# Chunk inverses: four link buffers, stores regrouped over SP and POOL, gate work moved, and dense products at every step of the joins

## What is computed

```python
T = jnp.where(tri, 0.0, -(kb @ jnp.swapaxes(k, -1, -2)))
for i in range(1, chunk):
    T = T.at[..., i, :].add(jnp.einsum('...j,...jl->...l', T[..., i, :], T))
T = T + jnp.eye(chunk, dtype=T.dtype)
u = T @ v
w = T @ kb
```

```python
ga = (2 * (ga >= 0) - 1) * jnp.maximum(jnp.abs(ga), 0.25)
gb = (2 * (gb >= 0) - 1) * jnp.maximum(jnp.abs(gb), 0.25)
```

## Time and profile before

| | us |
|---|---|
| median of 3 runs | 2583.9 (2582.48 to 2597.81) |
| the profiled execution | 2589.23 |
| its span | 2587.5 |
| PE busy in the span | 2394.4 (93%) |
| DVE busy | 1655.0 (64%) |
| ACT busy | 1109.5 (43%) |
| POOL busy | 616.3 (24%) |

### The profile page before, as it was taken

The page is one execution under the profiler, slowest core; times in us unless marked ns, Lnnn a source line. Parts: engine busy times, 40 slices in busy tenths (PEclk is TensorE's granted clock), DMA queues, the critical chain, the costliest instruction groups (busy, mean ns, idle before and its releaser), DMA issues.

```text
span 2587.5 us, 41994 instructions
## 1 busy us (share of the span) xinstructions
PE 2394.4 (93%) x14594; PEld 1659.7 (64%) x14594; DVE 1655.0 (64%) x4354; ACT 1109.5 (43%) x2350; POOL 616.3 (24%) x417
## 2 busy tenths in 40 slices
PE   6899997667897999979999999999999999999998
PEld 4466665555676888845666666666666666666665
DVE  4487886449922566525767676667667676766675
ACT  2477876346663222224334424433443344244331
POOL 1145554031101111211312231222123132312210
PEclk9999998787667999989999999999999999999999
DMA  5447556978767767421202210220122022101000
GB/s 166 162 149 219 174 166 192 270 212 203 212 155 223 217 204 225 156 74 49 58 1 58 58 50 9 58 58 13 45 59 58 1 58 58 43 15 58 9 9 8
DMA packets 376312, 272.14 MB, mean 105 GB/s; under 512 B 199714, under 2 KB 333794, under 8 KB 373906
## 3 DMA queue, kind: packets, MB, share of 16 engines
q1 hardware_dynamic: 371474, 243.85, 33.6%
q0 software_dynamic: 4640, 25.73, 2.9%
HBM read 168.60 MB, written 100.93 MB: 104 GB/s over the span
## 4 chain that ended last, share of the span: by engine, by line
PE 43%; DVE 9%; issue 3%; POOL 2%; ACT 0%; DMA 0%; DVEq 0%; SPq 0%; POOLq 0%; ACTq 0%
PE mx_dn L2002 16%; PE mx_up L1988 15%; PE mx_m L1938 4%; DVE mx_acc L2316 4%; PE mx_m L1965 2%; POOL mx_rms L1894 2%; PE mx_m L1942 1%; PE mx_m L1979 1%; DVE hl L2224 1%; DVE mx_st L2214 1%; DVE hl L2199 1%; DVE hl L2188 1%; DVE mx_rms L2193 1%; PE mx_m L1973 1%; PE mx_m L1947 1%
## 5 line engine op out<-in xcount | busy, mean ns | idle before, releaser
L2316 DVE SCALAR_TENSOR_TENSOR mx_acc<-mx_dn,mx_comb,mx_acc 128x256 f32<-128x256 f32 x1024 | 424.3, 478 | 356.6 <-PE mx_dn L2002 352.7
L2002 PE MATMUL mx_dn<-mx_edn,mx_hs 128*128 128x256 f32 x2048 | 487.7, 381 | 0.0
L1988 PE MATMUL mx_up<-mx_h2T,mx_eup 128*128 128x512 f32 x1024 | 484.3, 595 | 0.0
L2002 PEld LDWEIGHTS mx_dn<-mx_edn,mx_hs 128*128 128x128 f32 x2048 | 384.4, 190 | 145.6 <-issue 91.0
L2090 ACT ACTIVATE mx_hs<-mx_up 128x512 f32<-128x512 f32 x320 | 190.8, 596 | 625.8 <-PE mx_up L1988 625.1
L1988 PEld LDWEIGHTS mx_up<-mx_h2T,mx_eup 128*128 128x128 f32 x1024 | 190.9, 190 | 156.1 <-issue 145.2
L675 DVE SCALAR_TENSOR_TENSOR cv_acc<-cv_pre,conv_w,cv_acc 128x512 f32<-128x512 f32 x288 | 215.7, 750 | 78.2 <-ACT cv_acc L597 71.3
L539 PE MATMUL cv_pj<-cv_hT,wqkv 128*128 128x512 f32 x384 | 181.8, 604 | 12.7 <-ACT cv_acc L597 7.7
L713 POOL TENSOR_TENSOR rn<-cv_ss,half_pow 128x8 f32 x64 | 127.5, 1992 | 13.2 <-POOL cv_ss L709 13.2
L1880 POOL TENSOR_TENSOR mx_st<-mx_tmp,root_pow 128x24 f32<-128x24 f32 x30 | 124.6, 4168 | 20.1 <-DVE mx_tmp L2142 20.1
L1938 PE MATMUL mx_m<-mx_hT,wr 128*128 128x512 f32 x256 | 122.2, 601 | 3.3 <-DMA mx_x<-_attn_hidden_states_dram 2.5
(11 more groups left out here) (292 smaller groups left out, 3998.7 us busy)
## 6 DMA issues: line engine op xcount, KB each, us to landing
kqT_d<-cv_kqc SPq DMA_DIRECT2D x16, 1024.0 KB, 8.5
vf_d<-cv_vf SPq DMA_DIRECT2D x16, 1024.0 KB, 5.4
fl_toep<-taps_d SPq DMA_DIRECT2D x32, 392.0 KB, 7.3
ds_kqT<-kqT_d SPq DMA_DIRECT2D x10, 1024.0 KB, 5.9
fl_v<-vf_d SPq DMA_DIRECT2D x8, 1216.0 KB
ci_kT<-kqT_d POOLq DMA_DIRECT2D x19, 512.0 KB, 5.7
fl_d<-fl_out POOLq DMA_DIRECT2D x8, 1029.0 KB, 7.2
xin<-_attn_hidden_states_dram SPq DMA_DIRECT2D x16, 512.0 KB, 4.3
```

The costliest lines, as they stand in the source:

```text
L1988: ins = pe.matmul(up_ps[x % 2][:], lhs, h2T[i][:, k, :], start=(k == 0), stop=(k == KD - 1))
L2002: ins = pe.matmul(dn_ps[(i + n) % 2][:, j, :], hs[x % 4][:, j * P:(j + 1) * P], rhs, start=(x == 0 and j % 2 == 0) or x >= NS, stop=(x >= ...
L2316: ins = dve.scalar_tensor_tensor(out=acc[i][:, j, :], in0=dn_ps[(i + n) % 2][:, j, :], scalar=comb[i][:, j, e:e + 1], in1=acc[i][:, j, :], ...
```

## The change

- `link` gets four buffers in place of two, each with its semaphore.
- The order on SP: in the first eight steps, groups of three steps' stores (half, load of k, link), then three loads of blocks, then the fourth step's stores and the fourth load. Steps 8 to 10 are stored, then the blocks of step 12 loaded, then step 11 stored, then the blocks of steps 13 to 15 loaded, then `first_step`, then the halves of steps 12 to 15.
- The links of steps 12 to 15 are stored by POOL, behind its last stores of inverses.
- The loads of Wo and of the norm's weight go from SP's start to POOL, behind the last inverses. The gate work on DVE goes behind the last round of inversion, and `clamp_done` with its wait is dropped.
- The products in front of the four rounds become 30, 8, 8 and 40, all ahead of the wait for blocks. At the first tile of each other step PE waits for the Y copy of the tile before and issues 8.

```diff
-    K3 = 3 * Q
+    BUSY = (30, 8, 8, 40)
...
-        link = [sb(f"ci_link{i}", [P, B, H // 2, DK]) for i in two]
+        link = [sb(f"ci_link{i}", [P, B, H // 2, DK]) for i in range(RB)]
...
-                if p == 1:
-                    sp.wait_ge(clamp_done, 1)
...
-            for q in range(TB):
+            for q in range(0, 2 * ST, ST):
+                for i in range(ST - 1):
+                    put(q + i)
+                for i in range(ST - 1):
+                    load_blocks(q + ST + i)
+                put(q + ST - 1)
+                load_blocks(q + 2 * ST - 1)
+            for q in range(2 * ST, 3 * ST - 1):
+                put(q)
+            load_blocks(3 * ST)
+            put(3 * ST - 1)
+            for q in range(3 * ST + 1, TB):
+                load_blocks(q)
+            first_step()
+            for q in range(3 * ST, TB):
                 put_half(q)
-                if TB + KB + q < TB + 2 * ST:
-                    load_k(TB + KB + q)
-                if (q + RB) % ST == 0:
-                    put_link(q)
-                if q + RB < TB:
-                    load_blocks(q + RB)
-                if (q + RB) % ST:
-                    put_link(q)
-                if q == 3 * ST + 1:
-                    first_step()
...
+            pool.dma_start(prod[1][:].rearrange("p (k n) -> p k n", k=KD), w.Wo.rearrange("(k p) n -> p k n", p=P))\
+                .then_inc(wo_in, 16)
+            for i in two:
+                pool.dma_start(prod[0][i * DK:(i + 1) * DK, 0:1], w.o_norm_w.unsqueeze(1)).then_inc(wo_in, 16)
+            for q in range(3 * ST, TB):
+                put_link(q)
+            pool.wait_ge(last_link_out, 32 * ST)
...
                 if x % BT == 0:
                     if x:
                         pe.wait_ge(Y_done, x)
-                    busy(x, 6)
+                    busy(x, BUSY[x // BT])
+                elif b == 0:
+                    pe.wait_ge(Y_done, x)
+                    busy(x, 8)
                 if b == 0:
                     pe.wait_ge(blocks_in[q % RB], 16 * 6 * (q // RB + 1))
-                if x % BT == 0:
-                    busy(x, 8)
...
-                if b == 0 and q >= 2:
-                    act.wait_ge(link_out[q % 2], 32 * (q // 2))
+                if b == 0 and q >= RB:
+                    act.wait_ge(link_out[q % RB], 32 * (q // RB))
```

More of the change, by code:

```diff
@@ L930, in chunk_inverses @@
         gate_step = sem("ci_gate_step")
-        clamp_done = sem("ci_clamp_done")
         wo_in = sem("ci_wo_in")
@@ L952, in chunk_inverses @@
         half_out = [sem(f"ci_half_out{i}") for i in range(RB)]
-        link_out = [sem(f"ci_link_out{i}") for i in two]
+        link_out = [sem(f"ci_link_out{i}") for i in range(RB)]
+        last_link_out = sem("ci_last_link_out")
         block = ctx.enter_context(nc.Block("chunk_inverses"))
@@ L1053, in put_link, with put @@
                     sp.dma_start(m.link_d[step(q), :, :, 2 * e:2 * e + 2, :].rearrange("d b h c -> d b (h c)"),
[L1054 to L1060, removed]
+                                 link[q % RB][e * DK:(e + 1) * DK].rearrange("d b h c -> d b (h c)"))\
+                        .then_inc(link_out[q % RB], 16)
+            def put(q):
+                put_half(q)
+                if TB + KB + q < TB + 2 * ST:
+                    load_k(TB + KB + q)
+                put_link(q)
             for p in range(3):
@@ L1071, in _ @@
                 put_diag(3 * ST + i)
-            for q in range(TB):
-                put_half(q)
-                if TB + KB + q < TB + 2 * ST:
-                    load_k(TB + KB + q)
-                if (q + RB) % ST == 0:
-                    put_link(q)
-                if q + RB < TB:
-                    load_blocks(q + RB)
-                if (q + RB) % ST:
-                    put_link(q)
-                if q == 3 * ST + 1:
-                    first_step()
+            for q in range(0, 2 * ST, ST):
[13 more added lines that the diff above has]
+            for q in range(3 * ST, TB):
+                put_half(q)
             for i in range(RB):
                 sp.wait_ge(half_out[i], 16 * len(range(i, TB, RB)))
-            for i in two:
-                sp.wait_ge(link_out[i], 32 * (TB // 2))
+                sp.wait_ge(link_out[i], 32 * len(range(i, 3 * ST, RB)))
             sp.wait_ge(m.first_in, 16 * 5)
@@ L1113, in put_inverse, with put_link @@
                 pool.dma_start(rows_of(m.invT_d, FIRST[p], ST), Tt[:].rearrange("p e r c -> p (e r c)")).then_inc(T_out[p], 16)
+            def put_link(q):
+                pool.wait_ge(link_done, (q + 1) * B)
+                for e in two:
+                    pool.dma_start(m.link_d[step(q), :, :, 2 * e:2 * e + 2, :].rearrange("d b h c -> d b (h c)"),
+                                   link[q % RB][e * DK:(e + 1) * DK].rearrange("d b h c -> d b (h c)"))\
+                        .then_inc(last_link_out, 16)
             for n in range(KB):
@@ L1253, in keep_link @@
                 act.wait_ge(z_done, x + 1)
-                if b == 0 and q >= 2:
-                    act.wait_ge(link_out[q % 2], 32 * (q // 2))
-                act.activation(link[q % 2][:, b].rearrange("p h c -> p (h c)"), z_ps[:, 0:H // 2 * DK], ACT.Copy,
+                if b == 0 and q >= RB:
+                    act.wait_ge(link_out[q % RB], 32 * (q // RB))
+                act.activation(link[q % RB][:, b].rearrange("p h c -> p (h c)"), z_ps[:, 0:H // 2 * DK], ACT.Copy,
                                scale=-1.0).then_inc(link_done, 1)
@@ L1286, in _ @@
                     .then_inc(A_odd_done, 1)
[L1287 to L1308, removed]
             n = 0
@@ L1340, in _ @@
                 ins.then_inc(Tt_done, 1)
+            sign = Ad[1][:].rearrange("p e r c -> p (e r c)").rearrange("p (g b d) -> p g b d", g=2, b=B)
+            gate = (m.wog[:, :, 1, :], m.gbB[:])
+            for g in two:
+                dve.tensor_scalar(sign[:, g], gate[g], 0.0, 2.0, ALU.is_ge, ALU.mult).then_inc(gate_step, 1)
+                dve.scalar_tensor_tensor(out=gate[g], in0=gate[g], scalar=-1.0, in1=gate[g], op0=ALU.mult,
+                                         op1=ALU.max).then_inc(gate_step, 1)
+            dve.wait_ge(gate_step, 4)
+            for g in two:
+                dve.tensor_scalar(gate[g], gate[g], 0.25, None, ALU.max).then_inc(gate_step, 1)
+                dve.tensor_scalar(sign[:, g], sign[:, g], -1.0, None, ALU.add).then_inc(gate_step, 1)
+            dve.wait_ge(gate_step, 8)
+            for g in two:
+                ins = dve.tensor_tensor(gate[g], gate[g], sign[:, g], ALU.mult).then_inc(gate_step, 1)
+            dve.wait_ge(gate_step, 10)
+            dve.wait_ge(wo_in, 16 * 3)
+            for k in range(KD):
+                for b in range(B):
+                    ins = dve.scalar_tensor_tensor(out=m.wog[:, b, k, :], in0=prod[1][:, k * D:(k + 1) * D],
+                                                   scalar=prod[0][:, 0:1], in1=m.wog[:, b, 1, :], op0=ALU.mult, op1=ALU.mult)
+                ins.then_inc(wog_done, 1)
 def delta_scan(nc, m, w):
```

## The result

The changed kernel took 2620.2 us, the median of four runs (2614.1 to 2621.6), against 2583.2 for the kernel before beside it: 1.0118 of its time, interval 1.0091 to 1.0144, so 24 to 37 us more. The two medians lie 37.0 apart; the kernel before was later run beside the experiments, 19 to 25 times, with medians of 2585.4 to 2589.5, so some us of the 37 lie in the four runs of before. The forecast was 2604.0 with a range of 2584 to 2620: the time is at the range's upper end and outside the forecast's own narrower range of 2596 to 2612. The sign and what dominates were right, the size was too small. The time is that of the rival "the clock is lost before nearly every burst", but the profiled execution does not show that rival: six of its twelve step bursts met the full clock.

What follows compares the result with a forecast made beforehand. The joins' loop of PE and ACT was taken to bound the block. Terms summed to +7.8 us with the clock held, plus 12.6 for lost bursts: +20.4, median 2604, range 2584 to 2620 (its own 2596 to 2612).

Steps and rivals of the forecast that it cites:

- the clock is lost before nearly every burst: Rival on the step bursts: 12 x 2.4 + 7.8 = +37 us, 2620; chance 0.18.
- The bound: Chunk inverses block: the joins' loop, PE and ACT in turn, sets the end of the block.
- Gates at nothing: Gates moved behind the last round: the load of Ad is late next, so 0, bounds 0 and -0.7 us.
- The burst of 40: Products in front of round 3: 17.7 us at full clock from 758.2, giving a first join at 775.9.
- ACT sets the pace and the bursts hide: Rival on the joins: a 3.5 us backlog at each step's start hides the bursts; about -14 us, 2570; chance 0.12.
- Link waits, -17.2: Four link buffers: ACT's five waits for the link store go, -17.2 us.
- The regrouping, 0.9, 0.5 and 2.2 us of waits for blocks: Regrouped loads on SP: blocks land slightly behind PE at rounds 1 and 2 and at step 13.
- The tail, -1: Last link issue to the next block, 7.3 us: POOL's stores make it 4.2 to 8.3, taken as -1.
- A held step, 11.0 and 8.4: Step of four passes with its 3.5 us burst at full clock: 7.5 + 3.5 with grams, 4.9 + 3.5 without.
- Lost bursts, 7 times 1.8 = 12.6: Seven of 12 step bursts meet half clock, each 1.3 to 2.4 us over 3.5, middle 1.8; slow passes included.
- The wait of 2.2 for step 13's blocks: Round 3: blocks loaded behind step 11's link land at 786.5, PE is there at 784.3.

Runs made afterwards that it cites:

- gates_only: Kernel before with only the gate work and the loads of Wo moved behind the last inversion round; 2585.4 us, 0.9984 of the kernel before.
- new_bursts_only: Kernel before with only the change's bursts (30, 8, 8, 40 and 8 at each step), two link buffers, old store order; 2621.9 us, 1.0149.
- no_step_bursts: Changed kernel without the twelve bursts of 8 products at the steps; 30, 8, 8 and 40 stay; 2592.4 us, 1.0028 of the kernel before.
- no_bursts_only: Kernel before without the bursts in front of rounds 1 to 3; round 0 keeps 14 products, all ahead of the blocks; 2575.6 us, 0.9949.
- links_no_bursts: Kernel before with four link buffers and no bursts in front of rounds 1 to 3; 2568.0 us, 0.9917 of the kernel before.
- links_only: Kernel before with four link buffers and nothing else, old order on SP; 2577.1 us, 0.9967 of the kernel before.
- regrouped_no_bursts: Changed kernel without bursts in front of rounds 1 to 3 and at the steps, 14 products ahead of round 0; 2581.0 us, 0.9954 of the kernel before.
- old_bursts: Changed kernel with the old bursts (6 ahead of a round's blocks, 8 behind them, none at the steps); 2586.3 us, 0.9985 of the kernel before.
- blocks_earlier: Changed kernel with the old bursts, and blocks of steps 13 and 14 loaded ahead of step 11's stores; 2582.2 us, 0.9970 of the kernel before.
- last_burst_8: Changed kernel with 8 products in front of the last round in place of 40; 2614.4 us, 1.0106 of the kernel before.
- tail_burst: Changed kernel with ten more products behind the last link product; 2623.0 us, 1.0120 of the kernel before.

## Why the forecast was right in kind and short in size

- *The bound.* Right. PE's and ACT's joins end the block, and what lengthens them lengthens the block.
- *Gates at nothing.* Right: gates_only, and the first inverse waits for `Ad`.
- *The burst of 40.* Right as a size, 17.5 for 17.7. Its start was not: 773.0 in place of 758.2. The last load of step 12's blocks was issued at 776.3; with the 2.8 us to landing of the earlier trace rows that is about 780 (an estimate), so the last 10 us hid nothing.
- *ACT sets the pace and the bursts hide* (a rival, given 0.12). Refuted: ACT's wait for the joins grew from 38.5 to 88.8 us, and new_bursts_only is slower. In four pairs the kernel with fewer bursts was the faster one (no_step_bursts against after, no_bursts_only against before, links_no_bursts against links_only, regrouped_no_bursts against old_bursts, there with ratios whose intervals overlap).
- *Link waits, -17.2.* The step that failed first. The waits went, but links_only gained 10.9 in the block. A wait's length in the trace was taken as a gain in full. Of the other 6.3 us, 2.4 had not reached PE; what took the rest was not traced.
- *The regrouping, 0.9, 0.5 and 2.2 us of waits for blocks.* Not too small with the bursts in front, where after waits 1.4 us in one place. Too small as the price of the order by itself: old_bursts against links_only is +6.9 in the block (the gates in it are nothing), and +12.1 without bursts. The forecast held the landings against PE with each burst in front; the loads are late by more once PE is early.
- *The tail, -1.* Measured -0.2: from the last link copy to the next block 7.35 us (828.31 to 835.66), before 7.56 (802.05 to 809.61).
- *A held step, 11.0 and 8.4.* Measured 11.58 and 8.68. The burst is 3.69, not 3.5, and PE is idle 0.39 before it, for ACT's Y copy that the change makes it wait for. For the four held steps with grams that is some 2 us.
- *Lost bursts, 7 times 1.8 = 12.6.* In the profiled execution six were lost, at 2.5 each, 15.3: 2.7 more. The 7 came from no row, and other runs of the same bursts lost 8 to 11, so the runs that make up the median may have lost more than six. The middle of the range 1.3 to 2.4 was taken, but the far end was the right value: in the burst at 701.14 the mean clock is 0.61, so 4.7 of its 6.0 us were at half. And the passes ahead of it at half clock are not free, as the forecast had it: 651.62 to 663.90 is 12.28 for a step that takes 11.58, though its own burst held.

Round by round, held clock plus the bursts' 15.3, from a block start 1.7 earlier, gives 824.7 for the last link copy; it came at 828.3. Of the remaining 3.6, PE stood 1.9 inside a group of products at 737.9, with nothing there to wait for. The slow passes and the longer held step are in it too; they were not measured apart. The wait of 2.2 for step 13's blocks did not come, as PE was late itself.

Taken along one path of kernels, the block's +27.7 is: links -10.9, regrouping and gates +6.9, bursts of 30, 8, 8 and 40 for the old ones +8.9 (no_step_bursts less old_bursts), step bursts +22.8. In another order the shares differ: the bursts alone are +30.5 on before, and the rest then gives back 2.8. The +27.7 is 7.3 over the forecast's 20.4. The profile's other 10 us are the scan, which no term of the forecast had, and the blocks ahead and behind were 5.5 shorter. So in the profiled execution the miss has two parts: the bursts, held and lost, and a scan that the change did not touch. How the other runs' times divide is not known.

## What to carry to other kernels

Dense products that only raise TensorE's clock are paid in full where PE is on the path, and return only what PE was short of: compare a step with its burst at the full clock (11.6 us here) with one without it at half (10.4) before adding one, and try the kernel without those it has. A wait is not worth its length: find what is late next, and on a hand-written serial queue try the buffers and the new order apart, since here the first gained 11 us in the block and the second gave back 7 to 12. Before a standstill is put down to a wait, count which tile it is at: several of those above stand where the kernel waits for nothing. Do not count on a clock that is regained in one profile; the same code lost it at two of five bursts in one execution and at all five in another.

## What the runs showed of the hardware

The scan behind the block had two lengths over all fourteen profiles: 301.3 to 303.0 us in ten, 311.8 to 312.3 in four (after, last_burst_8, no_bursts_only, regrouped_no_bursts). Its instructions are the same in all. Windows of its start, first of before, then of after, then of no_bursts_only:

```profile
809.60:817.50 7.90, 5.85 (x45) 4.76 (x45) 3.12 (x8) 0.00 (x0) 3.36 (x8) 0.50 0.88 277
817.50:860.00 42.50, 42.50 (x474) 37.30 (x475) 23.71 (x63) 10.47 (x45) 6.97 (x12) 1.00 0.67 200
```

```profile
835.60:866.00 30.40, 27.95 (x177) 24.02 (x178) 9.60 (x25) 2.73 (x11) 8.00 (x16) 0.50 0.64 191
866.00:900.00 34.00, 34.00 (x390) 29.92 (x389) 19.52 (x53) 8.25 (x35) 2.32 (x4) 1.00 0.59 175
```

```profile
796.20:826.00 29.80, 27.77 (x176) 23.84 (x177) 9.60 (x25) 2.73 (x11) 8.00 (x16) 0.50 0.64 195
826.00:850.00 24.00, 24.00 (x268) 21.18 (x267) 13.41 (x37) 5.89 (x25) 2.33 (x4) 0.99 0.48 143
```

In the ten the clock rose within 10 us of the scan's start (8 in before), in the four about 30 us in, though PE had been busy 28 of those 30. Some 22 us more at half clock is about 11 us of PE's work (an estimate), the size of the difference. Kernels with the bursts and without them, with the old order on SP and the new, are in both groups, so the block's edits do not decide it, and tail_burst, whose products run up to the scan's start, had the early rise, which one profile cannot tell from chance. The runs of the kernel before reach from 2580 to 2607 us, wide enough for it, but of these only one has a profile. What decides between an early and a late rise stays open.

Second, a higher mean clock went with a longer block: 0.69 and 266.4 before, 0.85 and 294.1 after, 0.59 and 246.3 in links_no_bursts. Here the granted clock did not tell how soon the work was done.

Third, PE can stand still inside a group of products that needs no semaphore: 6.4 us in a join of regrouped_no_bursts, 3.7 in links_no_bursts, 1.5 to 2.9 in old_bursts and blocks_earlier, 1.9 in after. The view ends these with "issue", its word for nothing that the profile shows. It writes the same word on waits for blocks at a step's first tile. What causes them stays open.
